# Inverse square roots as a power on GpSimd, and a new merge order, in a fused attention and FFN kernel

## The reference

```python
h = layernorm(x) * (1 + ca) + sa
x = x + ga * attention(h)          # 16 heads of 8; softmax over k.v, applied to q
h = layernorm(x) * (1 + cb) + sb
x = x + gb * ffn(h)

def ffn(x):                        # two layers of this
    h = shift_token(x); q, k, v = split(h @ wqkv)      # 8 heads of 64
    q = q / max(norm(q), 1e-12) * q_scale              # the same for k
    q, k = rotary_xpos(q, k)
    x = x + local_attention(q, k, v) @ wo              # windows of 64, softmax
    h = shift_token(x)
    h = (h - mean(h)) / sqrt(var(h) + 1e-5) * ln_g + ln_b
    a, g = split(h @ w1 + b1)
    return x + (a * gelu(g)) @ w2 + b2
```

## Time and profile before

| what | us |
|---|---|
| three runs, median | 1195.36 |
| three runs, lowest and highest | 1194.01, 1196.31 |
| the profiled execution, its own time | 1196.15 |
| its span in the trace | 1194.3 |
| mean granted clock of PE over the span | 0.948 of full |

### The profile page before, as it was taken

How to read it: one execution, slowest core, us unless ns; L and a number is a source line. 1 busy time by engine, 2 the same in 40 slices (tenths; PEclk the granted TensorE clock), 3 DMA queues, 4 the chain that set the end, 5 groups by cost and what they waited for, 6 DMA issues and landing times. The chain is left out here.

```text
span 1194.3 us, 23996 instructions
## 1 busy us (share of the span) xinstructions
PE 997.0 (83%) x8124; PEld 510.0 (43%) x8124; DVE 949.4 (79%) x1947; ACT 918.2 (77%) x2782; POOL 508.1 (43%) x578
## 2 busy tenths in 40 slices
PE   2677787768888798778868897899999789999898
PEld 2232232223323352234336444655664357545664
DVE  4789898888869777986884699779769976789865
ACT  1698979899978988887659566868886587958983
POOL 5012143212105321343474058647823676348830
PEclk8699989999989898998989998999999999999999
DMA  5541305232204103001011001101110020001200
GB/s 206 180 142 36 106 1 146 62 107 71 72 0 130 43 28 115 10 10 24 1 31 34 10 1 32 33 1 32 33 41 10 10 63 16 18 1 32 46 20 27
DMA packets 28009, 59.18 MB, mean 50 GB/s; under 512 B 6192, under 2 KB 6384, under 8 KB 26736
## 3 DMA queue, kind: packets, MB, share of 16 engines
q1 hardware_dynamic: 27120, 56.33, 16.7%
q10 hardware_dynamic: 768, 1.31, 0.3%
HBM read 23.98 MB, written 18.87 MB: 36 GB/s over the span
## 5 line engine op out<-in xcount | busy, mean ns | idle before, releaser
L905 ACT ACTIVATE E<-psum,neg_max 128x512 f32<-128x512 f32 x512 | 346.6, 716 | 64.2 <-DVE neg_max L1191 45.9
L1191 DVE TENSOR_REDUCE neg_max<-psum 128x2 f32<-128x1024 f32 x256 | 307.5, 1214 | 58.7 <-PE psum L465 56.7
L465 PE MATMUL psum<-v_rows,k_rows 64*128 64x512 f32 x512 | 130.3, 514 | 106.0 <-ACT E L905 79.6
L998 ACT ACTIVATE rot_work<-psum,neg 128x128 f32<-128x128 f32 x512 | 184.3, 412 | 17.9 <-DVE neg L1284 11.0
L838 POOL TENSOR_TENSOR rot_work<-rot_work,rz 128x512 f32<-128x512 f32 x128 | 133.0, 1047 | 141.0 <-DVE rz L1289 140.9
L825 POOL TENSOR_TENSOR work<-work,rot_work 128x512 f32<-128x512 f32 x96 | 121.7, 1273 | 129.6 <-DVE rot_work L1262 129.3
L465 PEld LDWEIGHTS psum<-v_rows,k_rows 64*128 64x128 f32 x512 | 52.8, 196 | 250.6 <-ACT E L905 116.1
L803 POOL TENSOR_TENSOR qz<-qT,rz 128x32 f32<-128x32 f32 x128 | 30.8, 241 | 300.7 <-DVE rz L1195 299.8
L523 PE MATMUL psum<-wqkv_sb,hs 128*128 128x512 f32 x288 | 144.0, 622 | 6.8 <-DVE hs L1248 3.8
L474 PE MATMUL psum<-E,qz 128*32 128x512 f32 x1024 | 148.2, 653 | 0.2 <-POOL qz L803 0.2
L998 ACT ACTIVATION_READ_ACCUMULATOR rot_work<-psum,neg 128x1 f32 x512 | 126.7, 252 | 0.0
(11 more groups left out here) (140 smaller groups left out, 1784.7 us busy)
## 6 DMA issues: line engine op xcount, KB each, us to landing
k_rows<-k_scr SPq DMA_DIRECT2D x128, 64.0 KB, 1.9
work<-v_al SPq DMA_DIRECT2D x16, 512.0 KB, 4.4
v_rows<-v_scr SPq DMA_DIRECT2D x124, 64.0 KB, 1.9
work<-v_al SPq DMA_DIRECT2D x16, 384.0 KB, 5.7
k_scr<-hi SPq DMA_DIRECT2D x16, 256.0 KB, 3.0
k_scr<-lo SPq DMA_DIRECT2D x16, 256.0 KB, 3.3
v_scr<-hi SPq DMA_DIRECT2D x14, 256.0 KB, 2.9
v_scr<-lo SPq DMA_DIRECT2D x14, 256.0 KB, 3.1
```

The costliest lines, as they stand in the source:

```text
L465: pe.matmul(bank, k_rows[r:r + 64, half, hh, P * j:P * (j + 1)], v_rows[r:r + 64, b % 2, hh, :], start=True, stop=True).then_inc(full, 1)
L905: act.activation(E[:, (b * NG + g) % E_RING, 2 * half + m, :], pair[:, m], ACT.Exp, bias=neg_max[:, n, m:m + 1], accum_out=z[:, n, m:m + 1 ...
L998: last = act.activation(pr[s][:, u % PR_SLOTS, w, :], bank[:, 2 * W * w:2 * W * (w + 1)], ACT.Exp, bias=neg2[s][:, u, w:w + 1], accum_out= ...
L1191: dve.tensor_reduce(neg_max[:, n, :], pair, AX.X, ALU.max, negate=True).then_inc(max_ready, 1)
```

## The change

1. The inverse square roots are formed by POOL as a power with exponent -0.5: a `tensor_tensor` with `ALU.pow` whose second operand is a constant tile `minus_half`. For the heads POOL first does one `tensor_scalar` (maximum, then times 2^20). ACT's logarithm and exponential, DVE's clamp and all Newton steps go. DVE's normalization and POOL's scaling now wait for POOL's power.
2. POOL's generators get steps for this: in `a` one ahead of a batch's first `a_weigh`, for the next batch; in the streams one at entry, one after the fourth and one after the eighth `b_rotary` of a layer, one at a layer's end. The steps of DVE and ACT for it go.
3. All the strings of `ORDER` for PE, DVE, ACT and POOL, nearly all of SP's, and `BANKS` are new.

What the strings hold, by counting letters:

| engine | letters before / after | x steps ahead of the last a, before / after | first y, before / after (position) | first z, before / after |
|---|---|---|---|---|
| PE | 1166 / 1166 | 127 / 179 | 546 / 600 | 649 / 619 |
| DVE | 1116 / 1052 | 120 / 153 | 541 / 573 | 635 / 587 |
| ACT | 985 / 922 | 119 / 160 | 410 / 436 | 503 / 454 |
| POOL | 534 / 597 | 71 / 110 | 222 / 267 | 270 / 279 |

PE's steps of stream 0 are 376 for its four batches, 94 per batch, before and after.

```diff
-PREP_AT = {"var": 1, "rsqrt": 2, "normal": 4, "xT": 6, ...}
+PREP_AT = {"var": 1, "normal": 4, "xT": 6, ...}
-LN_CHAIN = 2 + 3
-B_CHAIN = LN_CHAIN + (2 * 2 + LN_CHAIN) * L
+LN_CHAIN = 2
+B_CHAIN = LN_CHAIN + LN_CHAIN * L
 ORDER = {
...
 (POOL)
-            pool.memset(clamp[:], SHIFT2).then_inc(s_clamp, 1)
+            pool.memset(minus_half[:], -0.5).then_inc(s_minus_half, 1)
+            def a_rsqrt(b):
+                pool.wait_ge(a_var, b + 1)
+                pool.tensor_tensor(rstd0[:], var_e[:], minus_half[:, :, 0], ALU.pow).then_inc(a_rstd, 1)
+            def b_enter_rsqrt(s, k):
+                pool.wait_ge(x2_var[s], k + 1)
+                pool.tensor_tensor(rstd1[s][:], var1[s][:], minus_half[:, :, 0], ALU.pow).then_inc(x2_rstd[s], 1)
+            def b_rsqrt(s, k, l):
+                pool.wait_ge(b_var[s], k * L + l + 1)
+                pool.tensor_tensor(rstd02[s][:], var2[s][:], minus_half[:, :, 0], ALU.pow).then_inc(b_rstd[s], 1)
             def a_stream():
                 for b in range(B):
                     for g in range(NG):
+                        if b + 1 < B and g == 0:
+                            a_rsqrt(b + 1)
+                            yield
+            def b_norm(s, k, l, w):
+                n = (k * L + l) * 2 + 2 - w
+                passed(pool, ss_ready[s], (k * L + l) * 2 * J + J * (2 - w))
+                pool.tensor_scalar(nt[s][:, :, w, :], ss[s][:, :, w, :], NORM_MIN2, SHIFT2, ALU.max, ALU.mult).then_inc(ss_all[s], 1)
+                pool.wait_ge(ss_all[s], n)
+                pool.tensor_tensor(rn[s][:, :, w, :], nt[s][:, :, w, :], minus_half[:], ALU.pow).then_inc(rn_ready[s], 1)
...
+            pool.wait_ge(s_minus_half, 1)
+            a_rsqrt(0)
             a_split(0, 0)
 (ACT)
-            def a_rsqrt(b):
-                act.wait_ge(a_var, b + 1)
-                act.activation(logs[:], var_e[:], ACT.Ln).then_inc(a_log, 1)
-                act.wait_ge(a_log, b + 1)
-                act.activation(rstd0[:], logs[:], ACT.Exp, scale=-0.5).then_inc(a_rstd, 1)
...
 (DVE)
-            def newton(v, r, t, link):
-                link(dve.scalar_tensor_tensor(t, v, -0.5, r, ALU.mult, ALU.mult))
-                link(dve.tensor_tensor(t, t, r, ALU.mult))
-                return dve.scalar_tensor_tensor(r, t, 1.5, r, ALU.add, ALU.mult)
...
```

More of the change, by code:

```diff
@@ L76 @@
[L76 to L80, removed]
@@ L189, in stream_tensors @@
                 r[n] = one(n, [P, J, 2])
-            for n in ("var1_", "logs1_", "rstd1_", "tmp1_", "var2_", "logs2_", "rstd02_", "tmp2_"):
+            for n in ("var1_", "rstd1_", "var2_", "rstd02_"):
                 r[n] = one(n, [P, J])
@@ L198, in stream_tensors @@
             r["v_al"] = one("v_al", [P, J, INNER])
-            for n in ("ss", "rn", "nt", "nlog"):
+            for n in ("ss", "rn", "nt"):
                 r[n] = one(n, [P, J, 2, H])
@@ L216, in build @@
             stats, mv = sa("stats", [P, J, 6]), sa("mv", [P, J, 2])
-            var_e, logs, rstd0, tmp4 = (sa(n, [P, J]) for n in ("var_e", "logs", "rstd0", "tmp4"))
+            var_e, rstd0 = (sa(n, [P, J]) for n in ("var_e", "rstd0"))
             qT = sa("qT", [D, 2, J, P])
@@ L236, in build @@
         stats1, mv1 = each("stats1_"), each("mv1_")
-        var1, logs1, rstd1, tmp1 = (each(n) for n in ("var1_", "logs1_", "rstd1_", "tmp1_"))
+        var1, rstd1 = (each(n) for n in ("var1_", "rstd1_"))
         stats2, mv2 = each("stats2_"), each("mv2_")
-        var2, logs2, rstd02, tmp2 = (each(n) for n in ("var2_", "logs2_", "rstd02_", "tmp2_"))
+        var2, rstd02 = (each(n) for n in ("var2_", "rstd02_"))
         y, hs, rot_work, work, v_al = (each(n) for n in ("y", "hs", "rot_work", "work", "v_al"))
@@ L248, in build @@
         up = [[v[:, n, :] for n in range(3)] for v in v_al]
-        ss, rn, nt, nlog = (each(n) for n in ("ss", "rn", "nt", "nlog"))
+        ss, rn, nt = (each(n) for n in ("ss", "rn", "nt"))
         kT, qT2 = each("kT"), each("qT2_")
@@ L843, in b_stream @@
                 for k in range(len(BATCHES[s])):
+                    enter_wait(pool, s, k)
+                    b_enter_rsqrt(s, k)
+                    yield
                     for l in range(L):
                         for n in range(2 * J):
-                            if (k, l, n) == (0, 0, 0):
-                                enter_wait(pool, s, k)
                             b_rotary(s, k, l, n)
                             yield
+                            if n == J - 1:
+                                b_norm(s, k, l, 1)
+                                yield
                             for i in {J: (0,), J + 1: range(1, J)}.get(n, ()):
@@ L852, in b_stream @@
                                 yield
+                        b_norm(s, k, l, 0)
+                        yield
                         for i in range(J):
@@ L931, in a_stream @@
                         if b + 1 < B:
-                            if n == PREP_AT["rsqrt"]:
-                                a_rsqrt(b + 1)
-                                yield
                             if n == PREP_AT["hT"]:
@@ L974, in b_values @@
                 act.activation(v_al[s][:, i, :], bank, ACT.Copy).then_inc(free, 1)
-            def b_norm(s, k, l, w):
-                act.wait_ge(ss_all[s], (k * L + l) * 2 + 2 - w)
-                act.activation(nlog[s][:, :, w, :], ss[s][:, :, w, :], ACT.Ln).then_inc(ss_log[s], 1)
-                act.wait_ge(ss_log[s], (k * L + l) * 2 + 2 - w)
-                act.activation(rn[s][:, :, w, :], nlog[s][:, :, w, :], ACT.Exp, scale=-0.5).then_inc(ss_rsqrt[s], 1)
             def b_heads(s, k, l, i):
@@ L1034, in b_stream @@
                                 yield
-                            if n == J + 1:
-                                b_norm(s, k, l, 1)
-                                yield
                             if n > J:
@@ L1040, in b_stream @@
                                 yield
-                        b_norm(s, k, l, 0)
-                        yield
                         b_keys(s, k, l, J - 1)
@@ L1064, in b_stream @@
                         yield
-            a_rsqrt(0)
             act.wait_ge(s_setup, 1)
```

151 lines of the change are left out of this document (60 added, 91 removed).

## The result

The changed kernel takes 1314.24 us (median of 4 runs, 1313.27 to 1319.19) against 1195.57 for the kernel before (4 runs): a ratio of 1.1003, with a 95% interval of 1.0973 to 1.1032. It is 10% slower; the forecast was 1161.

What follows compares the result with a forecast made beforehand. ACT and DVE were taken to bound attention, PE mostly the rest. Attention's end at 603.4 plus 556.5 behind it gave a 1159.9 us span; with 1.85 outside it and 0.8 to the median, 1161 us, range 1140 to 1198.

Steps and rivals of the forecast that it cites:

- The stretches and the order: Span cut at attention's end; more stream work merged into attention: attention ends at 603.4 us, 556.5 follow.
- the relief: Root steps removed from DVE and ACT, net of POOL's additions: 8 us gained behind attention, 5 in it.
- The order's 21.4 us: Merge order alone: 46.6 us added to attention, the rest falls from 632.5 to 564.5 us, a gain of 21.4.
- stream 2 enters at once: At attention's end: stream 2 enters within 10 us, so the two-stream stretch at 107 us a batch is gone.
- the order only moves work: Rival behind attention: pace stays at 98 us a batch, time 1194 us, no change; chance 0.16.
- the share of the chain: Behind attention: removed steps lie on the chain as often as their engine at large, 23.6 us DVE, 1.9 ACT.
- Added to POOL: POOL's powers and max-and-multiply steps: 59 us busy, 1.3 us per 128x32 power, 17.7 us on the chain.
- Its idle half covers it: On POOL: the added 59 us, raising busy time from 508 to 567, is covered by its idle half.
- The slow power: Rival in POOL's queue before scaling: each us above 1.3 adds 11.5, slower than before past 4.3; chance 0.13.
- A late first power: Rival before the first layer norm: POOL fetches something first, 1162 us, or 1167 by code loading; chance 0.2 inside the forecast.
- POOL's new waits in attention: In POOL's attention queue: the wait at a_rsqrt is free, and b_norm's 1.3 us power fits behind E's three buffers.

Runs made afterwards that it cites:

- free roots: Changed kernel with every power made a multiplication by a constant, roots left out, so it only tells time: 1141.18 us; the same in the old order: 1169.30 us.
- ACT's pair: Heads' roots by ACT's logarithm and exponential alone, no Newton step, layer norms by POOL's power: 1158.11 us in the new order, 1169.76 in the old.
- the old roots in my places: New order with the earlier roots, ACT's pair placed 0.7 us and DVE's Newton step 1.4 us behind the clamp: 1237.83 us.
- Old order and free roots: Old merge order with POOL's steps of the change, each power a multiplication, roots left out: 1169.30 us, ratio 0.9768 to the kernel before.
- Newton alone: Kernel before with DVE's three Newton instructions at each of 64 roots removed, ACT's pair and old order kept: 1171.47 us, ratio 0.9799.
- free heads: Changed kernel with the heads' power made a multiplication, roots left out, and the layer norms' power of 128x4 kept: 1146.96 us.
- the later places: New order with the earlier roots, ACT's pair 1.0 us and DVE's Newton step 2.5 us behind the clamp: 1251.12 us.
- the half one: Changed kernel with the heads' power formed for two of four token columns, the other two multiplied by a constant: 1228.29 us.

## Why the prediction was wrong

**The stretches and the order: right in the sum, one step wrong.** With a 0.25 us step for the power, attention ends at 597.1 and 542.6 us follow, forecast 603.4 and 556.5; with so cheap a step my own sum has 545 for the second (see the relief). The order's 21.4 us measured 28 (1169.3 to 1141.2) with free roots, 16 and 12 with powers and with ACT's pair, and a loss of 42 with the old roots in my places. But "stream 2 enters at once" failed: it enters 29 us behind attention's end, so for that long two streams run and not three. At 107 against 92.6 us a batch that is worth some 4 us, an estimate from the same rows, so the miss is small beside the others. The rival that the order only moves work is refuted for free roots.

**The relief: right.** The earlier trace rows add up to 78.8 us of DVE, and DVE lost 64: steps of one engine overlap in the rows, so such a sum runs high (all of DVE's groups in the kernel before add to 1031 us against 949.4 busy). In time the share of the chain gave 23.6 + 1.9 behind attention, and I took 5 in it. With a cheap step for the power POOL has 21 us more busy time, which my share prices at 0.36 x 6.65/8 x 21 = 6 us. That makes 19 behind attention and 5 in it. Old order and free roots measured 19 and 6. The parts fit less well: Newton alone gave 24 us where the share gave 18.

**"Added to POOL": the step that failed, twice.**
The term held 17.7 us for all that POOL took on; the powers alone measured 173 (1141.2 to 1314.2).

First the size: I took 1.3 us between 0.24 and 3.5, "near a plain POOL step over 16 times the columns". 5.45 us lies above my upper end. That end was a memset, and neither end was a price of arithmetic of this kind: a bound from rows of other work bounded nothing.

Second the share: I priced a us of power at the share that the removed DVE steps had on the chain, 0.36, so 11.5 us of kernel per us on each of the 32 (the sum itself took 6.65/8 of that, which I left out in the rival). The table shows 28 us per us up to 2.9, and 32 up to 5.45 and 10.9: nearly the whole of it. A share of the chain is how often small steps of an engine happened to stand there. It says nothing of a step twenty times as long in a queue behind which the scaling, the rotation and the weighing of all streams wait. "Its idle half covers it" was the same error, and the idle time shows it: 607 us with free roots, 595 with the powers, 597 with each head power doubled. POOL waits for inputs in that time (in the kernel before, 299.8 us for DVE's reciprocal in attention alone), and the head powers did not go into it: each starts when its inputs are there, with its followers due. The layer norms' powers did: with them and free heads the idle time is 588 us.

**The slow power, my rival at 0.13, is what happened,** with its place right and its slope wrong by three. It gave 1161 + 4.15 x 11.5 = 1209 for 5.45 us; measured 1314. It put the turning point at 4.3 us. By the line from 1147 to 1228 the 1195 of before are reached at 0.25 + 48.4/28 = 2.0 us, an estimate, and my own upper bound of 3.5 lay beyond that. Had I priced a us of power at its whole length, 32 us, my own 3.5 us would have given 1161 + 2.2 x 32 = 1231 (counting only what lies above 1.3), outside my range of 1140 to 1198.

**A late first power: refuted.** DVE's variance, POOL's first power and DVE's normalization in order of time:

```profile
10.54 0.17 DVE L1139 TENSOR_SCALAR var_e<-mv 128x4 f32<-128x4 f32 x1
10.87 1.03 POOL L795 TENSOR_TENSOR rstd<-var_e,minus_half 128x4 f32<-128x4 f32 x1 [2.10 <-DVE var_e L1139]
11.94 1.11 DVE L1143 TENSOR_SCALAR xn<-x_sb,mv,rstd 128x128 f32<-128x128 f32 x4 [1.22 <-POOL rstd L795]
```

It starts 0.16 us after its input and takes the usual 1.03 us; the first exponential starts at 37.3 instead of 36.9. So the rule of the Trainium skill, "GPSIMD Engine Reference", § 2.1 Instruction dispatch, of some 6 us at the first call of a freshly loaded kernel, did not apply to this power: the trace disagrees for it.

**POOL's new waits in attention: wrong.** I called a power of 1.3 us behind three buffers harmless. With 5.45 us attention grew from 560.1 us (free) to 612.9: 53 us, for some 42 us more of head powers and 10 of the others. The buffers aren't where most of it shows. PE waits 9 us there for POOL's weighing, but 26 us for POOL's scaling of stream 0 (L854, ahead of L529), and PE's string has attention's scores behind those transposes. DVE's maximum, which exists in attention alone, stands for them longer, first with the powers, then with free roots:

```profile
DVE neg_max L1179 <- PE psum L464: 90.5, 79, 10.4
...
DVE neg_max L1179 <- PE psum L464: 51.5, 71, 10.7
```

So the wait that I looked for in POOL's queue came mostly by PE's.

**What stays open.** Why the new order with the old roots is 43 us slower than before: place or order. POOL's scalings wait 67 us in all for DVE's roots there and 85 us with the later places, where it was 27 in the kernel before; that points to the place, but no run has it by itself. How much of the powers' price comes by PE's lower granted clock (0.97 over the span with free roots, 0.905 with the powers) is not split either; it may be why the longer powers cost 32 us per us and the half one 28. And why Newton's removal is worth more than its share of the chain; that small DVE steps stood still beside POOL's fits, but was not tried by itself.

## What to carry to other kernels

Before work is moved to an idle engine, ask whether the engine is idle for want of work or for want of inputs; in the second case a moved step can stand in front of everything the inputs release, and then costs its whole length times its count. Where it doesn't, as with the layer norms' powers here, it can still hide, so the place has to be tried and not only the engine. A price with no row of its kind has no upper bound from rows: compute at what price the change turns, and let the range reach past it. Ask also whether the work is needed: dropping the Newton step and keeping two ACT instructions won what the power was meant to win.

## What the runs showed of the hardware

A two-input power on GpSimd in float32 took 1.02 us for 4 columns of 128 partitions, 1.65 for 8, 2.92 for 16 and 5.45 for 32, all within 0.02 us of 0.38 us + 0.158 us per column. A product of 128x32 took 0.25 us in the same place. Plain products took 0.25 us for 32 columns and 1.04 us for 512 (L854), 0.0016 us per column, so a column of the power costs about a hundred times as much (an estimate from these rows).

The granted clock of PE was lower where PE waited more: 0.97 in attention and 0.99 behind it with free powers, 0.90 and 0.92 with real ones, and the doubled power's kernel had 0.865 over its span. The matmuls of L529 on `work` took 279 ns on average with free powers, 315 with real ones and 322 with doubled ones.
